# Attention inside a two-layer kernel: the values' two parts in one stationary tile, a PSUM bank per head, and both halves added in the output projection

## The reference

```python
# 2 sequences of 512 tokens, hidden size 256, 32 query heads, 8 key/value heads, head size 64
q = rope(x @ Wq.T); k = rope(x @ Wk.T); v = x @ Wv.T       # k, v repeated over 4 query heads
p = softmax(causal(q @ k.T / 8))
out = (p @ v) @ Wo.T
```

## Time and profile before

| | |
|---|---|
| time, median of 3 runs | 772.52 us (769.67 to 774.16) |
| time of the profiled execution | 774.21 us |
| its span in the trace | 772.4 us |
| attention, first score to last | 345.9 to 742 us |
| one middle group (20 steps) | 48.87 us |
| granted TensorE clock, mean | 0.982 |

### The profile page before, as it was taken

How to read it: one execution, slowest core, us unless ns; L and a number is a source line. 1 busy time by engine, 2 the same in 40 slices (tenths; PEclk the granted TensorE clock), 3 DMA queues, 4 the chain that set the end, 5 groups by cost and what they waited for, 6 DMA issues and landing times.

```text
span 772.4 us, 13448 instructions
## 1 busy us (share of the span) xinstructions
PE 716.3 (93%) x4575; PEld 625.0 (81%) x4576; DVE 487.4 (63%) x1030; ACT 416.8 (54%) x1043; POOL 397.1 (51%) x449
## 2 busy tenths in 40 slices
PE   2999999999999998588789999999999999999995
PEld 2887989989989986566678888888888888888883
DVE  7582655334332437876557777777777778777764
ACT  4446244134144133447367777667766677667663
POOL 1412442422332323118577786767867778677460
PEclk9899999999999999899899999999999999999999
DMA  8075977776877744154134222332223322232001
GB/s 295 31 249 183 277 251 233 246 245 203 280 241 214 244 98 118 27 168 121 60 94 112 58 63 65 84 89 52 64 63 90 85 55 64 52 90 56 1 1 55
DMA packets 103828, 98.06 MB, mean 127 GB/s; under 512 B 50576, under 2 KB 74064, under 8 KB 103632
## 3 DMA queue, kind: packets, MB, share of 16 engines
q1 hardware_dynamic: 101648, 91.43, 40.8%
q0 software_dynamic: 2112, 5.77, 2.3%
HBM read 69.24 MB, written 11.14 MB: 104 GB/s over the span
## 4 chain that ended last, share of the span: by engine, by line
PE 63%; DVE 12%; POOL 10%; ACT 8%; issue 4%; SPq 2%; DMA 1%; DVEq 0%; ACTq 0%; POOLq 0%
PE bank L1656 14%; PE bank L1516 8%; PE bank L1690 7%; PE bank L1517 7%; PE bank L1518 7%; PE bank L1512 7%; POOL prob L1474 5%; ACT prob L1290 3%; PE bank L1796 3%; DVE nmax L1035 2%; PE bank L1797 2%; POOL q_lo L1486 2%; ACT p_hi L1297 2%; DVE o_lo L1048 1%; POOL wq_lo L1454 1%
## 5 line engine op out<-in xcount | busy, mean ns | idle before, releaser
L1474 POOL TENSOR_TENSOR prob<-prob,rinv 128x128 f32<-128x128 f32 (+3 forms) x256 | 177.6, 724 | 102.9 <-DVE rinv L1040 102.9
L1290 ACT ACTIVATE prob<-bank,nmax 128x512 f32<-128x512 f32 (+3 forms) x256 | 133.2, 528 | 45.3 <-DVE nmax L1035 43.8
L1044 DVE TENSOR_TENSOR p_lo<-bank,p_hi 128x512 fp32r<-128x512 f32 x160 | 110.0, 687 | 52.8 <-ACT p_hi L1297 51.9
L1297 ACT ACTIVATE p_hi<-bank 128x512 fp32r<-128x512 f32 x160 | 96.3, 602 | 79.3 <-PE bank L1512 79.3
L1656 PEld LDWEIGHTS bank<-xgT,wm 128*128 128x128 f32 x920 | 108.7, 192 | 4.5 <-issue 2.9
L1656 PE MATMUL bank<-xgT,wm 128*128 128x128 f32 x920 | 111.3, 275 | 0.5 <-ACT xgT L1199 0.5
L1512 PE MATMUL bank<-cst,prob 128*128 128x128 f32 x640 | 97.9, 276 | 3.0 <-POOL prob L1474 1.2
L1035 DVE TENSOR_REDUCE nmax<-bank 128x1 f32<-128x512 f32 (+2 forms) x192 | 91.0, 502 | 12.7 <-PE bank L1799 12.1
L1516 PE MATMUL bank<-p_hi,v_lo 128*128 128x128 f32 (+3 forms) x256 | 93.0, 363 | 0.3 <-DVE p_lo L1044 0.3
L1796 PE MATMUL bank<-kT,qT 128*128 128x512 f32 (+3 forms) x256 | 82.2, 326 | 11.6 <-ACT prob L1290 6.0
L1445 POOL DMA_INDIRECT y_rows<-y_row,to_row x21 | 22.7, 1081 | 118.3 <-DVE y_row L904 92.6
(11 more groups left out here) (307 smaller groups left out, 1544.6 us busy)
## 6 DMA issues: line engine op xcount, KB each, us to landing
wm<-in_w_moe SPq DMA_DIRECT2D x23, 1280.0 KB
wm<-in_w_moe SPq DMA_DIRECT2D x23, 640.0 KB
qT<-q_hi SPq DMA_DIRECT2D x124, 64.0 KB, 2.0
qT<-q_lo SPq DMA_DIRECT2D x124, 64.0 KB, 2.0
k_exp<-k_rows SPq DMA_DIRECT2D x56, 64.0 KB, 2.0
wtl<-in_w_moe_tail SPq DMA_DIRECT2D x46, 64.0 KB
y_rows<-gate SPq DMA_DIRECT2D x1, 2048.0 KB, 14.1
wq_raw<-in_w_qkv SPq DMA_DIRECT2D x32, 64.0 KB, 2.5
```

The lines of the kernel that those rows point to most:

```text
L1044: TT(p_lo[:, b_, :], bank[2 + b_ % 2][:, :], p_hi[:, b_, :].bitcast(F32), ALU.subtract).then_inc(plo_done, 1)
L1290: ins = actv(prob[:, i % 2, h, POFF[j]:POFF[j] + (j + 1) * P], bk[:, at:at + (j + 1) * P], ACT.Exp, bias=nmax[:, i % 2, h, j:j + 1], accum ...
L1297: actv(p_hi[:, b_, :], bank[2 + b_ % 2][:, :], ACT.Copy).then_inc(phi_done, 1)
L1474: ins = GT(seg, seg, rinv[:, i % 2, k, j:j + 1].to_broadcast([P, (j + 1) * P]), ALU.mult)
```

## The change

- The values are kept as `v_parts = [upper | lower | upper]`, without zeros. For head 0 the stationary slice is `[upper | lower]`, for head 1 `[lower | upper]`. One matmul gives the product with the upper part of the values in one half of the partitions and the product with the lower part in the other. A piece is so two matmuls (by `p_lo` and by `p_hi`) instead of three.
- Each head has a bank of its own, 4 or 5, the same for every pair. The order of the pieces in `TURNED` is another: head 0 is complete at the third step of a pair, head 1 at the fifth. One piece of head 1 is written as two matmuls of 256 columns.
- O is done twice a pair, once for each head, one step after that head's last piece. ACT copies the 64 partitions of the upper product into `o_hi`; DVE makes `bank - o_hi` on those 64 partitions and a copy of the other 64 (a `scalar_tensor_tensor` with a column of -1 and 0) into `o_rest0` or `o_rest1`.
- W has 8 matmuls instead of 6: two with the weights `wo_twice`, in which the 64 rows of a head stand in both halves of the partitions, so that the product adds the halves; and two with `wo_lo` and `wo_hi` as before, all for each of the two pairs.
- SP fills `wo_twice` by four transfers a group (`double_wo`), placed before the load of the next output weights. W waits for them.
- The four zero fills of the padding on POOL become one, of `o_hi`; DVE writes four small constants at the program's start.

```diff
-TURNED = [[(0, 0, 0)], [(0, 1, 0), (0, 3, 3 * P)], [(1, 0, 0)], [(1, 1, 0), (1, 3, 3 * P)], [(0, 2, 0), (1, 2, 2 * P)]]
+TURNED = [[(0, 0, 0)], [(0, 1, 0), (0, 3, 3 * P)], [(0, 2, 0), (1, 2, 2 * P)], [(1, 0, 0)], [(1, 1, 0), (1, 3, 3 * P)]]
+VALUED = (2, 4)
+VALUED_BY = {(1, 0): [(0, 2 * P), (2 * P, HALF)]}
...
-        own += [(5 * r + 4 + LAG + TO_V + 1, 1, "O", r, 0)]
+        own += [(5 * r + VALUED[h] + LAG + TO_V + 1, 1, "O", r, h) for h in range(2)]
...
+            def double_wo(g):
+                sp.wait_ge(wohi_done, g + 1)
+                for h in range(2):
+                    for to in range(2):
+                        sp.dma_start(wo_twice[to * HD:(to + 1) * HD, :, h, :].bitcast(F32),
+                                     wo_hi[h * HD:(h + 1) * HD, :, :].bitcast(F32)).then_inc(twice_in, 16)
...
                 load_v(g + 1, 1)
+                double_wo(g)
                 load_wo(g + 1)
...
-                        dve.wait_ge(ohi_done, q + 1)
-                        TT(o_lo[:, b, m, :], bank[4 + m][:, :], o_hi[:, b, m, :].bitcast(F32), ALU.subtract).then_inc(olo_done, 1)
+                        dve.wait_ge(ohi_done, 2 * q + k + 1)
...
+                        to = o_rest1[:, m, :] if k else o_rest0[:, b, m, :]
+                        STT(out=to, in0=o_hi[:, b, m, :].bitcast(F32), scalar=minus[:, k:k + 1], in1=bank[4 + k][:, :],
+                            op0=ALU.mult, op1=ALU.add).then_inc(olo_done, 1)
...
-                        actv(o_hi[:, b, m, :], bank[4 + m][:, :], ACT.Copy).then_inc(ohi_done, 1)
+                        if k == 1:
+                            act.wait_ge(olo_done, 2 * q + 1)
+                        hs = slice(k * HD, (k + 1) * HD)
+                        actv(o_hi[hs, b, m, :], bank[4 + k][hs, :], ACT.Copy).then_inc(ohi_done, 1)
...
-                actv(v_hi[:, ts, HD:2 * HD], v_all[:, ts, 0:HD], ACT.Copy).then_inc(vhi_done, 1)
+                upper_v(ts, v_all[:, ts, 0:HD])
...
                         if k == 0:
-                            pe.wait_ge(olo_done, q + 1)
                             if i % 2 == 0:
                                 pe.wait_ge(vlo_done, g * 2 + (b + 1))
+                            if q > 0:
+                                pe.wait_ge(olo_done, 2 * q - 1)
+                        if k == VALUED[0] and q > 0:
+                            pe.wait_ge(olo_done, 2 * q)
...
-                            ins = split3(dst, v_hi[:, b * TB + j, vs], v_lo[:, b * TB + j, vs], p_hi[:, b_, at:at + n],
-                                         p_lo[:, b_, at:at + n], k == 0, last)
+                            vs = v_parts[:, b * TB + j, h * HD:(h + 2) * HD]
+                            for p, first, end in ((p_lo, True, False), (p_hi, False, True)):
+                                for x, y in VALUED_BY.get((h, j), [(j * P, HALF)]):
+                                    ins = mm(bank[4 + h][:, x:y], vs, p[:, b_, at + x - j * P:at + y - j * P],
+                                             start=first and (h, j) in ((0, 0), (1, 2)), stop=end and (h, j) in ((0, 2), (1, 3)))
...
+                        pe.wait_ge(twice_in, (g + 1) * 64)
...
-                            ins = split3(bank[6 + m][:, :], wo_hi[:, c, m * P:(m + 1) * P], wo_lo[:, c, m * P:(m + 1) * P],
-                                         o_hi[:, b, c, :], o_lo[:, b, c, :], c == 0, c == 1)
+                            mm(dst, wo_twice[:, c, 0, ms], o_rest0[:, b, c, :], start=c == 0, stop=False)
+                            mm(dst, wo_twice[:, c, 1, ms], o_rest1[:, c, :], start=False, stop=False)
+                            mm(dst, wo_lo[:, c, ms], o_hi[:, b, c, :], start=False, stop=False)
+                            ins = mm(dst, wo_hi[:, c, ms], o_hi[:, b, c, :], start=False, stop=c == 1)
```

More of the change, by code:

```diff
@@ L194, in layered_kernel @@
         ab = sb("ab", [P, KC], F32)
+        minus = sb("minus", [P, 2], F32)
         low = (nc.sbuf_base + 31) // 32 * 32
@@ L374, in layered_kernel @@
         o_hi = attn("o_hi", [P, 2, 2, HALF], F32R)
-        o_lo = attn("o_lo", [P, 2, 2, HALF], F32R)
+        o_rest0 = attn("o_rest0", [P, 2, 2, HALF], F32R)
+        o_rest1 = attn("o_rest1", [P, 2, HALF], F32R)
         def k_mix(r, b):
@@ L625, in _ @@
             load_v(1, 1)
+            double_wo(0)
             load_wo(1)
@@ L642, in _ @@
             move_q(KVH - 1, 1)
+            double_wo(KVH - 1)
             for b in range(BATCH):
@@ L701, in _ @@
             then(vec.memset(chosen[:, NT, :], 0.0))
+            for h in range(2):
+                then(vec.memset(minus[h * HD:(h + 1) * HD, h:h + 1], -1.0))
+                then(vec.memset(minus[(1 - h) * HD:(2 - h) * HD, h:h + 1], 0.0))
             vec.memset(ptl[0:TAIL, :, :], 0.0).then_inc(pad_zero, 1)
@@ L1046, in attend @@
                         b, m = i // 2, i % 2
-                        dve.wait_ge(ohi_done, q + 1)
-                        TT(o_lo[:, b, m, :], bank[4 + m][:, :], o_hi[:, b, m, :].bitcast(F32), ALU.subtract).then_inc(olo_done, 1)
+                        dve.wait_ge(ohi_done, 2 * q + k + 1)
+                        if q == 0:
+                            dve.wait_ge(o_zero, 1)
+                        if k == 1 and m == 0 and q > 0:
+                            dve.wait_ge(wo_full, g * (BATCH * KC) + 2 * b + 1)
+                        to = o_rest1[:, m, :] if k else o_rest0[:, b, m, :]
+                        STT(out=to, in0=o_hi[:, b, m, :].bitcast(F32), scalar=minus[:, k:k + 1], in1=bank[4 + k][:, :],
+                            op0=ALU.mult, op1=ALU.add).then_inc(olo_done, 1)
                     elif op == "W":
@@ L1268, in upper_q, with upper_v @@
                 actv(q_hi[:, :, :], q_mix[:, :, 0, :], ACT.Copy).then_inc(qhi_done, 1)
+            def upper_v(ts, src):
+                return actv(v_parts[:, ts, :].rearrange("p t (a d) -> p t a d", a=3)[:, :, 0:3:2, :],
+                            src.unsqueeze(2).to_broadcast([P, TB, 2, HD]), ACT.Copy).then_inc(vhi_done, 1)
             def upper_k(now, i):
@@ L1299, in attend @@
                         b, m = i // 2, i % 2
-                        act.wait_ge(av_done, q * 5 + 9)
-                        if m == 0 and not (isinstance(g, int) and b * KC + g * (BATCH * KC) <= 1):
+                        act.wait_ge(av_done, q * 5 + VALUED[k] + 5)
+                        if q == 0:
+                            act.wait_ge(o_zero, 1)
+                        if k == 0 and m == 0 and g > 0:
                             act.wait_ge(wo_full, g * (BATCH * KC) + (b * KC - 1))
-                        actv(o_hi[:, b, m, :], bank[4 + m][:, :], ACT.Copy).then_inc(ohi_done, 1)
+                        if k == 1:
+                            act.wait_ge(olo_done, 2 * q + 1)
+                        hs = slice(k * HD, (k + 1) * HD)
+                        actv(o_hi[hs, b, m, :], bank[4 + k][hs, :], ACT.Copy).then_inc(ohi_done, 1)
                     elif op == "VO":
@@ L1323, in attend @@
                         act.wait_ge(av_done, now * STEPS + (10 * i - 6))
-                        actv(v_hi[:, ts, HD:2 * HD], v_exp[:, ts, :], ACT.Copy).then_inc(vhi_done, 1)
+                        upper_v(ts, v_exp[:, ts, :])
                     elif op == "F":
@@ L1447, in _ @@
             gp_.wait_ge(row_full, NJ)
-            for v in (v_hi, v_lo):
-                for z in (0, 2):
-                    pool.memset(v[:, :, z * HD:(z + 1) * HD].bitcast(F32), 0.0).then_inc(vpad_ready, 1)
+            pool.memset(o_hi[:, :, :, :].bitcast(F32), 0.0).then_inc(o_zero, 1)
             def split_wq(g):
```

24 lines of the change are left out of this document (9 added, 15 removed).

## The result

| | before | after |
|---|---|---|
| time, median of 4 runs | 772.51 us (769.67 to 774.16) | 784.65 us (783.75 to 785.43) |
| ratio, with its 95% interval | | 1.0152 (1.0122 to 1.0181) |
| span of the profiled execution | 772.4 us | 783.6 us |
| one middle group | 48.87 us | 50.03 us |
| first score of the first group to that of the second | 60.83 us | 61.26 us |

The change costs 12 us. In the span it is 11.2 us: six middle groups 7.0, the last group 1.9, the tail 1.9, the first group 0.4.

What follows compares the result with a forecast made beforehand. It took DVE and ACT to bound the light part (steps 5 to 9), PE only the heavy part (steps 0 to 4). Terms 3.4 + 1.7 + 1.3 + 0.5 + 0.5 = +7.4 us on 772.5 gave 780.0 us, range 765 to 793.

Steps and rivals of the forecast that it cites:

- The light part is paced by DVE and ACT, not PE: Steps 5 to 9 of each half group: the added O lengthens them by 0.71 us; PE's 1.26 us saving becomes idle time.
- O at step 1 is covered by W: Heavy part, steps 0 to 4: the new DVE operation costs nothing behind W on PE; uncovered it would cost 0.66 us.
- The heavy part gets shorter by 0.33 + 0.10 us: Steps 0 to 4: A saves 1.26 us, W adds 0.93, and 0.10 less waiting for POOL, per half group.
- O at step 8 costs +0.05: Light part, second stretch: the new DVE form replaces the old one and takes 0.05 us more.
- ACT's additional copy is hidden: Step 6: ACT's second copy falls while DVE is in the rotary half, costing nothing; its price would be about 0.5 us.
- Both halves alike: Middle groups: one half group's sum, +0.28 us, was taken for all twelve halves.
- Middle groups +3.4 us: Six middle groups, twelve halves at +0.71 - 0.33 - 0.10 = +0.28 us each; bounds +0.06 to +0.7 a half.
- First group +3.0: First group: W waits 1.7 us for the doubled weights' transfers, and two more O in its second half add 1.3 us.
- Last group +0.5, tail +0.5: Last group: new O partly in gaps, +0.5 us (-2.5 to +2); tail: last two W longer by 0.93, A shorter, +0.5.
- PE is the bound after all: Rival, whole kernel: all 25.6 us of PE's saved work come through, 747 us; chance 0.14.
- The added O is mostly covered: Rival, step 6: DVE finds time for the new O, so the heavy part's gain stands alone, 769 us; chance 0.16.
- the clock falls: Rival: PE idling in light parts lowers its clock, next heavy part starts at half pace, +16 us, 796; chance 0.05.

Runs made afterwards that it cites:

- the spare operation: Kernel before, plus one unused DVE maximum over 128x512 ahead of the row maxima of steps 1, 6, 11 and 16: 780.4 us, ratio 1.0088.
- the small O: Changed kernel with DVE's O of head 0 handling 8 columns instead of 512, all else as it was: 778.5 us, ratio 1.0068.
- the last run: Changed kernel with ACT's wait for DVE's O of head 0 made one step earlier, before p_hi: 783.7 us, ratio 1.0137.

## Why the prediction was right

It said 780.0 us (its terms add up to 779.9), 765 to 793, slower with 0.64; the time is 784.65. The mechanism of the forecast is the one that the runs show, and all of its signs came but one, the wait of the first group's W for a transfer. The sizes are worse than the total: the middle groups, the last group and the tail came to 10.8 us where the sum has 4.4, and the first group to 0.4 where it has 3.0. That the second error took 2.6 us off the first is luck. Term by term:

- *The light part is paced by DVE and ACT, not PE.* Right. S(5) to S(8) grew to 6.18 us (5.52 + 0.66 = 6.18 by its terms), the new O had no idle time before it, and PE's waits for ACT rose to 35.7 us (it said some 25). The two runs that add and remove one DVE operation at this place show the cause alone: +0.61 and -0.54 us a half group.
- *O at step 1 is covered by W.* Right: the spare operation stood there too, the half group grew by one only, and its heavy part by nothing.
- *The heavy part gets shorter by 0.33 + 0.10 us.* Right within 0.05: by 0.39 us on the mean of both halves (0.48 in one, 0.30 in the other). The 0.10 us for POOL stands on no run of its own; the wait for POOL in this part is what held the gain back in later runs.
- *O at step 8 costs +0.05.* Too small: +0.20 (4.31 against 4.11 us). The term was taken from the length of the DVE operation; ACT's copy before it also lost its overlap with its neighbours.
- *ACT's additional copy is hidden.* It is about as long for half the partitions (0.594 us, the median of 64, against 0.606 us before), and by the timeline it is hidden at step 6.
- *Both halves alike.* The sum costed one half and doubled it, and it was the half of steps 15 to 20 (the rows it reads start at 494.31). There S(15) to S(18) is 6.40 us, 0.22 more than the 6.18 that came out in steps 5 to 8. In its rows ACT's `wo_hi` stands at 544.57, ahead of a `p_hi`, and DVE's rotary half starts only after S(15). With the small O the same 0.21 us is there (5.87 against 5.66), so DVE's O of head 0 is not its cause; no run isolated another.
- *Middle groups +3.4 us.* Mis-sized: +7.0. With +0.15 in every half (O at step 8) and +0.22 in every second, 0.26 a half is missing from the sum, 12 x 0.26 = 3.1 of the 3.6 us; the heavy part's 0.04 is most of what remains.
- *First group +3.0: a wait for the doubled weights, 1.7, and two O, 1.3.* Wrong: +0.4. This is the step of the sum that failed as a mechanism; the other misses are of size. In the changed kernel W starts without waiting:

```profile
403.58 2.63 SPq L596 DMA_DIRECT2D wo_twice<-wo_hi  x4
406.25 0.59 SPq L602 DMA_DIRECT2D wo_raw<-in_w_o  x1
...
408.27 0.47 PE L1863 MATMUL bank<-o_rest,wo_twice 128*128 128x512 f32 x1
```

  (and of the page's transfers, in the columns of the earlier trace rows:)

```profile
wo_twice<-wo_hi SPq DMA_DIRECT2D x32, 128.0 KB, 2.5
```

  I had put the four transfers behind the load at its place before, 405.23. But SP had come there late because everything ahead of it was late, and in the changed kernel that was earlier: the transfers ahead of them start 0.55 us earlier (400.02 against 400.57) and the four of `k_exp` take 2.44 us instead of 3.52. The doubled weights are issued from 403.58 to 406.21, and with 2.5 us to landing they are there at about the time of W. What moved all that earlier no run has told apart. It was close: in six variants of the changed kernel the first W does wait for these transfers, 0.7 to 1.9 us, and in the one with DVE's O moved it is the 1.94 us above, near the 1.7 of the sum. That wait falls after the first score of the second group, so it would not show in the 0.4. The two O in this group cost nothing visible.
- *Last group +0.5, tail +0.5.* Too small: +1.9 and +1.9. The last group holds the same added O (the bounds reached to +2), and the tail two W of eight matmuls and one O more. No run took these two apart.

Of the rivals, "PE is the bound after all" needed the group to fall; with the same saving and nothing added it fell by a third of the saving. "The added O is mostly covered" fails at the row without a gap. The clock did not fall in the middle groups of the changed kernel, and the doubled weights were late in none of them. And the occupancy rule that the prediction weighed (the Trainium skill, Perfetto Trace Analysis, Identifying the Most-Contended Engine: work on the engine of highest occupancy) would have chosen PE, with 93% busy and 81% by its weight loads, over DVE with 63%. Here that view and the measured worth of its work differ: 41 us of matmuls (8 groups of 5.1) gave 9.6 us, while moving one DVE operation per pair, with no work saved, gave 8.8. The measurement decides.

Of the kernels here that leave nothing of the result out, the fastest is the one before with DVE's O moved behind E: 763.8 us, or with the whole O moved, 763.9.

## What to carry to other kernels

Ask of every operation added to a less busy engine in which row of that engine it stands and whether that row has a gap there, since its share over the span (63% here) says nothing of it; an operation of 0.6 us in the wrong place cost its whole length each time, where 0.6 us of matmuls gave 0.2. Try a change of place before a change of amount: moving O by a few entries in the list gave 8.8 us without touching the arithmetic. And when PE's saving is taken beside added work elsewhere, measure the saving alone first, as its worth here was a third.

## What the runs showed of the hardware that I had not expected

**Here a copy at partitions 64 to 127 did not overlap its neighbours on ACT.** In the middle groups, 24 times of 24, `o_hi` of head 0 (partitions 0 to 63) starts 0.10 to 0.14 us before its predecessor's end and is followed, where the next is ready, after 0.48 us; that of head 1 (partitions 64 to 127) starts 0.02 us after it and is followed after 0.62 us. The kernel before, which copies all 128 partitions, starts it 0.11 to 0.13 us before its predecessor's end. First head 0, then head 1, of the changed kernel:

```profile
523.56 0.19 ACT L1316 ACTIVATION_READ_ACCUMULATOR prob<-bank,nmax 128x1 f32 x1
523.65 0.58 ACT L1335 ACTIVATE o_hi<-bank 64x512 fp32r<-64x512 f32 x1
524.13 0.58 ACT L1323 ACTIVATE p_hi<-bank 128x512 fp32r<-128x512 f32 x1
...
528.55 0.22 ACT L1316 ACTIVATION_READ_ACCUMULATOR prob<-bank,nmax 128x1 f32 x1
...
529.41 0.60 ACT L1323 ACTIVATE p_hi<-bank 128x512 fp32r<-128x512 f32 x1
```

It costs about 0.15 us on either side. The wait is excluded as the cause by the last run; the place of the partitions is what remains different, but no run changed it alone, so the cause is argued and not shown.

**The clock can fall in a middle group.** In the run with the queries a step earlier PE was idle for 2.41 us before the first score of one group (515.20); towards the end of that idle time the granted clock fell, and then (columns as above):

```profile
512.80:515.10 2.30, 0.00 (x0) 0.00 (x0) 0.69 (x2) 2.25 (x6) 0.00 (x0) 0.92 0.14 36
515.10:518.00 2.90, 2.81 (x11) 2.32 (x12) 2.58 (x7) 1.91 (x7) 2.73 (x5) 0.50 0.46 112
518.00:521.00 3.00, 3.00 (x20) 2.63 (x18) 1.62 (x4) 1.69 (x5) 3.00 (x4) 0.97 0.19 45
```

It ran at 1.2 GHz for 2.9 us, where a matmul of 512 columns of the scores took 0.56 us from start to start instead of 0.31. PE has twelve idle times of 2.39 to 2.41 us in this run, one before S(10) and one before S(20) of each middle group, and only at this one did the clock fall; what made it different no row shows. The heavy part behind it took 15.68 us instead of 14.33, so it cost 1.35 us. So the rival "the clock falls" was nearer than its 0.05 may sound: the changed kernel idles 1.4 us at a time, this one 2.4. In the changed kernel's first group it did fall, from 395.9 to 402.7 us, after an idle time of 2.47 us and within one of 1.80 that came soon after; the kernel before, with 1.10 and 1.80 us idle at the same two places, kept its full clock there.
